# A graph kernel's step in another order, its score row spread through DRAM, its 512-column products halved

## The reference, cut to what matters

```python
def L0(X, A, Wv, bv, aw, ab, Wk, bk):        # K = 3
    Xw = X @ Wv + bv
    sj, si = Xw @ aw[:d, 0], Xw @ aw[d:, 0]
    e = leaky_relu(sj[:, None, :] + si[:, :, None] + ab[0], 0.2)
    alpha = A * exp(e)
    T = alpha / (sum(alpha, -1, keepdims=True) + 1e-12)
    H, Xk = 0, X
    for k in range(3):
        H = H + Xk @ Wk[k] + bk[k]
        Xk = T @ Xk
    return relu(H)

def gcn(x, adj, W, b):
    return adj @ (x @ W) + b

h = relu(layernorm(x));  x = x + L0(h, adj, ...)
h = relu(layernorm(x))
x = x + gcn(relu(gcn(relu(gcn(h, adj, W1, b1)), adj, W2, b2)), adj, W3, b3)
```

## Time and profile before

| what | value |
|---|---|
| median of 3 runs | 836.76 us (836.75 to 837.14) |
| the profiled execution | 837.53 us |
| its span, first to last instruction | 835.4 us |
| TensorE busy | 818.7 us, 98%, 6219 matmuls |
| VectorE busy | 718.0 us, 86% |
| ScalarE busy | 684.0 us, 82% |
| GpSimd busy | 506.8 us, 61% |
| mean granted TensorE clock | 0.997 of full |

### The profile page before, as it was taken

One profiled execution on the slowest core, in us unless ns is written; L12 is line 12 of the kernel. 1 busy time (PEld: TensorE's weight loads), 2 busy tenths in 40 slices (PEclk: granted clock), 3 DMA queues, 4 the chain that ended last, 5 costly groups with the idle time before them and its releaser, 6 DMA issues.

```text
span 835.4 us, 20996 instructions
## 1 busy us (share of the span) xinstructions
PE 818.7 (98%) x6219; PEld 772.0 (92%) x6219; DVE 718.0 (86%) x2001; ACT 684.0 (82%) x1673; POOL 506.8 (61%) x591
## 2 busy tenths in 40 slices
PE   7899999999999999999999999999999999999996
PEld 6799999999999999999999999999999999999995
DVE  6989889888889889889889889889888889889882
ACT  4788888888888888888888888888888888888774
POOL 3475665665665665665665665665665665665553
PEclk9999999999999999999999999999999999999999
DMA  7144334334344334334334334334334344344101
GB/s 195 43 99 107 86 95 103 91 94 104 88 95 102 92 93 103 92 93 110 84 93 108 87 93 106 87 94 106 88 94 105 85 97 109 83 95 102 46 27 38
DMA packets 245064, 77.54 MB, mean 93 GB/s; under 512 B 202324, under 2 KB 237016, under 8 KB 244952
## 3 DMA queue, kind: packets, MB, share of 16 engines
q1 hardware_dynamic: 243864, 75.16, 37.5%
q10 hardware_dynamic: 1088, 1.05, 0.4%
HBM read 43.39 MB, written 32.77 MB: 91 GB/s over the span
## 4 chain that ended last, share of the span: by engine, by line
PE 95%; ACT 1%; DVE 1%; DMA 1%; issue 1%; POOL 1%; ACTq 0%; DVEq 0%; POOLq 0%
PE bank L984 44%; PE bank_p L984 37%; PE bank_turned L984 7%; PE bank_T L984 5%; PE bank_T L1003 2%; DMA w_raw<-in_L_gnn_Wk 1%; POOL w_p_lo L422 0%; ACT y_full L614 0%; ACT h L490 0%; POOL y__lo L392 0%; PE bank_p L1160 0%; ACT y__hi L614 0%; DVE stats L693 0%; DVE alpha L766 0%; ACT y_hi L569 0%
## 5 line engine op out<-in xcount | busy, mean ns | idle before, releaser
L392 POOL TENSOR_TENSOR y__lo<-y_full,y__hi 128x256 fp32r<-128x256 f32 x256 | 183.6, 737 | 131.4 <-ACT y_full L614 131.4
L383 POOL TENSOR_TENSOR rstd<-veps,minus_half 128x2 f32<-128x2 f32 x128 | 111.6, 872 | 184.9 <-DVE veps L710 184.9
L984 PE MATMUL bank_p<-w_p_hi,h0T_hi 128*128 128x258 f32 (+1 forms) x512 | 176.3, 361 | 0.2 <-DVE y_full L795 0.2
L984 PE MATMUL bank_p<-w_p_lo,h0T_hi 128*128 128x258 f32 (+1 forms) x512 | 165.7, 339 | 0.0
L984 PE MATMUL bank_p<-w_p_hi,h0T_lo 128*128 128x258 f32 (+1 forms) x512 | 142.5, 340 | 0.0
L984 PE MATMUL bank<-w_gcn_hi,y__hi 128*128 128x256 f32 x512 | 130.2, 290 | 2.1 <-ACT y__hi L614 1.3
L984 PE MATMUL bank<-w_gcn_lo,y__hi 128*128 128x256 f32 x512 | 123.7, 278 | 0.0
L614 ACT ACTIVATE y__hi<-bank,bias_col 128x256 fp32r<-128x256 f32 x256 | 119.9, 468 | 3.6 <-PE bank L984 3.5
L614 ACT ACTIVATE y_full<-bank,bias_col 128x256 f32<-128x256 f32 x256 | 120.6, 471 | 0.0
L984 PEld LDWEIGHTS bank_p<-w_p_hi,h0T_hi 128*128 128x128 f32 x512 | 97.1, 190 | 6.5 <-issue 0.4
L984 PEld LDWEIGHTS bank_p<-w_p_lo,h0T_hi 128*128 128x128 f32 x512 | 97.6, 191 | 6.0
(11 more groups left out here) (100 smaller groups left out, 2285.4 us busy)
## 6 DMA issues: line engine op xcount, KB each, us to landing
x_in<-in_x SPq DMA_DIRECT2D x64, 256.0 KB, 3.0
x_new<-x_out SPq DMA_DIRECT2D x64, 256.0 KB, 2.2
h_rows<-h SPq DMA_DIRECT2D x61, 256.0 KB, 2.0
h_blocks<-h_rows SPq DMA_DIRECT2D x244, 64.0 KB, 2.6
adj_blocks<-in_adj SPq DMA_DIRECT2D x256, 32.0 KB, 2.0
w_raw<-in_L_gnn_Wk ACTq DMA_DIRECT2D x3, 256.0 KB, 6.9
w_raw<-in_L_gnn_W SPq DMA_DIRECT2D x3, 256.0 KB, 3.5
wv_raw<-in_L_gnn_Wv ACTq DMA_DIRECT2D x1, 256.0 KB, 3.8
```

The source lines that it names most:

```text
L383: pool.tensor_tensor(rstd[n][k % 2][:], veps[n][k % 2][:], minus_half[:], ALU.pow)\
L392: pool.tensor_tensor(y[n][1][:, c], y_full[n][:, c], plain(y[n][0][:, c]), ALU.subtract)\
L984: return pe.matmul(dst, stationary, moving, start=start, stop=stop, skip_group_check=True)
```

## The change

- The score row no longer goes through two transposes on TensorE but, from pair 3 on, through DRAM: SyncE writes one column of uv as 256 single numbers (`write_scores`) and reads them back broadcast to 128 partitions (`read_scores`); the logits read that tile in SBUF instead of bank_T.
- TensorE's order becomes p2 of a, ay of b, z1 of c, z3 of d, p01 graph 0 of a, s2 of c, p01 graph 1 of a, z2 of c, m of b, ap of a, s3 of c. z1 thus moves from the end of a round behind ay of the next. Rounds 0 to 2 keep the transposes; the filling in the last rounds is dropped.
- Each 512-column product of p01 is two of 256 with the same left operand.
- The lists of ScalarE, VectorE, GpSimd and SyncE are reordered to match. y1 is signalled graph by graph, and the high part of p2 waits graph by graph. ay runs its low part last and waits for y1_lo only there. s3, and the low parts of s2 and s3, wait chunk by chunk. GpSimd waits for y1_lo ahead of adjT_lo.

The diff, cut to its core:

```diff
+            def write_scores(i, k):
+                sp.wait_ge(uv_made, i + 1)
...
+                sp.dma_start(v_rows[k % 2].rearrange("g (n o) -> n g o", o=1), uv[k % 2][:, :, 1:2],
+                             allow_slow_non_contiguous=True).then_inc(v_out[k % 2], 16)
+            def read_scores(i, k):
+                sp.wait_ge(v_out[k % 2], scores_seen(i))
...
+                sp.dma_start(v_bc[k % 2][:], v_rows[k % 2].rearrange("(o g) n -> o g n", o=1)
+                             .to_broadcast([P, G, P])).then_inc(v_landed[k % 2], 16)
...
+                if spread is not None:
+                    write_scores(i, k)
+                    read_scores(i, k)
...
+                if b is not None:
+                    y1_high(b, kb)
+                if d is not None:
+                    s3_high(d)
                 if a is not None:
                     scores_copy(a, k)
                     p2_high(a, k)
+                if (n := next_norm(i)) is not None and after(i, 3):
+                    first_norm(n, n % ROUND)
+                if c is not None and i != 3:
+                    layer_result(0, c)
+                if (n := here(i, -1)) is not None and n > ON_TENSOR + 1:
+                    hT_high(n, n % ROUND)
+                if a is not None and a >= SPREAD_ON_TENSOR:
+                    logits(a, k)
+                    exponentials(a, k)
+                if c is not None:
+                    s2_copy(c)
+                if b is not None and after(i, 3):
+                    norm(b, kb)
                 if a is not None:
                     aT_high(a, k)
+                    if after(i, 2):
+                        p1_copy(a, k, 0)
                 if c is not None:
                     layer_result(1, c)
                 if a is not None:
                     p1_copy(a, k, 1)
...
+                if c is not None and after(i, 3):
+                    m_low(c)
+                if b is not None and after(b, 1):
+                    y1_low(b, kb)
+                if b is not None:
+                    p0_bias(b, kb)
+                if d is not None and after(d, 1):
+                    s3_low(d)
                 if b is not None:
                     h_sum(b, kb)
                     residual(b, kb)
                     x1_statistics(b, kb)
+                if nxt is not None and nxt > ON_TENSOR:
+                    turn_rows(nxt, kn)
...
-                        last = matmul(bank_p[:, g, :], h0T[k % 2][a][:, g, c, :], w_p01[b][:, c, :],
-                                      c == 0 and (a, b) == (HI, HI), c == C - 1 and a == LO)
+                        for n in range(2):
+                            cols = slice(n * D, (n + 1) * D)
+                            last = matmul(bank_p[:, g, cols], h0T[k % 2][a][:, g, c, :], w_p01[b][:, c, cols],
+                                          c == 0 and (a, b) == (HI, HI) and n == 0, c == C - 1 and a == LO)
...
+                if b is not None and after(i, 3):
+                    ay_product(b, kb)
+                if c is not None and after(i, 4) and not tail(i):
+                    z1_product(c)
+                if d is not None:
+                    z3_product(d, kd)
+                if a is not None and (first(i) or after(i, 3)):
+                    p01_product(a, k, 0)
+                if c is not None:
+                    s2_product(c)
                 if a is not None:
                     p01_product(a, k, 1, (0,))
                     p01_product(a, k, 1, (1,))
+                if c is not None:
+                    z2_product(c, kc)
+                if b is not None:
+                    m_product(b, kb)
+                if a is not None:
                     ap_product(a, k)
                 if c is not None:
                     s3_product(c)
```

More of the change, by code:

```diff
@@ L43 @@
 ON_TENSOR = 3
+SPREAD_ON_TENSOR = 3
 LN_EPS = 1e-5
@@ L209, in gnn_kernel @@
         spread_done = sem("spread_done")
+        v_out = [sem(f"v_out{k}") for k in range(2)]
+        v_landed = [sem(f"v_landed{k}") for k in range(2)]
         z_made = sem("z_made")
@@ L622, in one @@
                     p01_weights_high()
[L623 to L628, removed]
+                if b is not None:
+                    y1_high(b, kb)
+                if second(i):
+                    first_norm(2, 2)
+                if d is not None:
+                    s3_high(d)
                 if a is not None:
@@ L640, in one @@
                         hT_high(2, 2)
+                if first(i) or second(i):
                     p1_copy(a, k, 0)
+                if a is not None and a >= SPREAD_ON_TENSOR:
[3 more added lines that the diff above has]
+                    s2_copy(c)
+                if i == ON_TENSOR:
+                    hT_high(ON_TENSOR + 1, 0)
+                if b is not None and after(i, 3):
+                    norm(b, kb)
                 if i == 2:
                     adjT_high(0, 0)
-                if b is not None:
+                if b is not None and not after(i, 3):
                     norm(b, kb)
@@ L942, in one @@
                     attention(a, k)
+                if d is not None:
+                    finish(d, kd)
+                if a is not None and after(i, 2):
+                    p2_low(a, k)
                 if second(i):
                     hT_low(2, 2)
-                if nxt is not None and nxt >= ON_TENSOR:
+                if nxt == ON_TENSOR:
                     turn_rows(nxt, kn)
@@ L948, in one @@
                     aT_low(a, k)
-                if d is not None:
-                    finish(d, kd)
+                if (n := next_moments(i)) is not None:
+                    shift(0, n, n % ROUND)
                 if nxt is not None:
                     turn_adj(nxt, kn)
+                if second(i):
+                    m_low(b)
                 if a is not None:
@@ L1020, in h_low_ready, with times_weights @@
                     pe.wait_ge(hT_lo, i - ON_TENSOR + 1)
-            def times_weights(hT, rows, w, cols, dst, starts, passes=(False, True)):
-                steps = [(g, c, a, b) for low in passes for g in range(G) for c in range(C)
+            def times_weights(hT, rows, w, cols, dst, graphs, starts, passes=(False, True)):
+                steps = [(g, c, a, b) for low in passes for g in graphs for c in range(C)
                          for a, b in PARTS if (a == LO) == low]
@@ L1073, in ay_product @@
             def ay_product(i, k):
-                pe.wait_ge(y1_lo, i + 1)
-                pe.wait_ge(z_made, i + 1)
-                for g in range(G):
-                    for a, b in PARTS:
+                pe.wait_ge(y1_hi, i + 1)
+                pe.wait_ge(z_made, min(i + 1, SPREAD_ON_TENSOR))
+                if after(i, 1):
+                    pe.wait_ge(h_made, i)
+                for a, b in ((HI, HI), (LO, HI), (HI, LO)):
+                    if b == LO:
+                        pe.wait_ge(y1_lo, i + 1)
+                    for g in range(G):
                         last = matmul(ay_ps[:, g, :], aT[k % 2][a][:, g, :], y1[k % 2][b][:, g, :],
-                                      g == 0 and (a, b) == (HI, HI), a == LO)
+                                      g == 0 and (a, b) == (HI, HI), b == LO)
                 last.then_inc(ay_done, 1)
@@ L1115, in z1_product, with low_by_chunk @@
                 last.then_inc(z_done[0], 1)
+            def low_by_chunk(n, i, w, dst):
+                for c in range(C):
+                    pe.wait_ge(y_lo[n], C * i + c + 1)
+                    for g in range(G):
+                        last = matmul(dst[g], y[n][LO][:, c, g, :], w[HI][:, c, :], False, c == C - 1)
+                return last
             def s2_product(i):
```

210 lines of the change are left out of this document (112 added, 98 removed).

## The result

The changed kernel takes 1457.02 us (median of 4 runs, 1454.05 to 1461.24) against 836.91 (836.75 to 837.14): ratio 1.741, 95% interval 1.738 to 1.7445. The forecast was 819, range 812 to 838. The changed kernel is slower by 620 us, far outside the range, and far beyond the 885 given to the rival that named the cause.

What follows compares the result with a forecast made beforehand. TensorE was taken to bound the kernel, never waiting in a steady round. From the profiled 837.5 us, -19.5 for 61 shorter rounds and +1.0 for the ends gave 819.0 us, range 812 to 838.

Steps and rivals of the forecast that it cites:

- the rival that named the cause: The DRAM round trip of the score row becomes the new bound: slower, 885 us at 2.8 us a half; chance 0.16.
- What bounds the kernel now: Steady rounds: TensorE never waits, 12.53 us busy of 12.53; only its matmul sum or a new wait moves the time.
- The sum of the new round on TensorE: TensorE's matmul start distances per round: 12.21 us against 12.53, so -0.32, or -19.5 us in 61 rounds.
- The term for the halving: p0/p1 on TensorE: 24 products at z1's 0.1133 us, 2.72 against 2.80, -0.08 us a round.
- The price of the round trip: SyncE's write and read of the score row: 2.0 us each plus 0.1 hand-over, 4.1 us, covered up to about 4.6.
- the bound of 6.5: Upper bound given for the DRAM round trip of the score row; the lower was 4.0 us.
- rival A: Loop through the DRAM trip, 7.6 + D, sets the round: 849 us at D = 5.1, 885 at 5.7; chance 0.16.
- D: Time of the score row's round trip through DRAM, write, read and hand-over, ahead of the logits; forecast 4.1 us.
- Does the new order keep TensorE fed: Walk through the engines' queues: nothing stalls by the sum, but all covers are only 0.2 to 0.5 us thick.
- rival B: A 0.2 us cover (s3's low parts, z1's results, alpha) missed by 0.1 to 0.25 us each round: 825 to 834; chance 0.20.
- the lock with alpha: VectorE's alpha beside GpSimd's h0T_lo: 1.25 us instead of 0.69, ending about 8.4 instead of 8.2, before aT_hi's 8.8.
- Ends: First and last rounds: round 1 adds 0 (-1 to +1), the end +0.6 and +0.4; +1.0 us in all.

Runs made afterwards that it cites:

- order_shift: order_only with the second norm's shift moved right behind the statistics of x and the first norm's variance guard behind finish; 837.05 us, ratio 0.9992.
- split_only: The kernel before with only the 512-column products of p0/p1 halved to 256 columns; 837.9 us, ratio 1.001.
- order_shift_512: order_shift with the 512-column products left whole; 837.87 us, ratio 1.001.
- write_apart: The changed kernel with the 256 four-byte pieces written 512 bytes apart and the read taking a KB of bias bv; 870.51 us.
- read_apart: read_only with each partition reading its own KB of x instead of all 128 the same one; 872.24 us.
- read_only: The changed kernel with the score row written in rounds 3 and 4 alone, the read kept in each round; 877.5 us.
- after: The profile of the changed kernel itself, with nothing further altered; 1457.02 us, ratio 1.741 to the kernel before.
- filled: The changed kernel with 64 idle-filling transposes in TensorE's wait ahead of z2, from round 4 on; 1340.11 us.
- order_only: The changed kernel without the DRAM round trip: score transposes stay on TensorE behind z3, new order and halved products kept; 861.56 us, ratio 1.028.
- n_major: The changed kernel with the DRAM score row laid out node by node instead of graph by graph, same 256 four-byte pieces; 1335.09 us.

## Why the prediction was wrong, point by point

**What bounds the kernel now: right.** TensorE without idle; only a smaller sum or a new wait could move the time, and a new wait did.

**The sum of the new round on TensorE: right but for one term.** 12.21 was forecast without the transposes. With them, 0.23, it is 12.44, and order_shift measured 12.447. The term for the halving was too large: -0.08 was taken from z1's rows, 0.02 and 0.00 were measured. The Trainium skill's 262 for 518 cycles (TensorE: Matmul & The Clock Gate, Back-to-back issue gap), by the prediction's estimate +1.8 us, was nearer: split_only shows +1.1 with nothing within its interval, order_shift against order_shift_512 -0.8; the rows had said -4.9. The trace had a second sign: the first pair of a group costs 0.33 whatever its form, so part of the 12 products could not gain.

**The price of the round trip: the step that failed.** "I take 2.0 each" came from rows that were near in the wrong respect. The write of h is a write to DRAM, but in long rows; the bias columns are 4-byte pieces, but read from DRAM. Neither has 4-byte pieces *into* DRAM side by side, and that they lie side by side makes the price: write_apart writes the same pieces apart in 1.6 us (median), under the forecast's 2.0, where the changed kernel takes 7.9. So the bound of 6.5 was a bound on other transfers. The text said that no row showed a small write to DRAM and yet closed the range at 2.8 a half; a range that honoured it had to stay open above. The read was mis-sized too, at 2.0: it lands after 5.1 (median), of which 2.1 is the read, 1.0 that all read one KB, and 2.0 comes with the write ahead of it (read_apart, read_only, after). The Trainium skill's rule of read, modify and write below 512 bytes (DMA: Bandwidth & Descriptors, Specifications) had spoken for rival A; write_apart's pieces are as small, and its 1.6 us show nothing extra.

**Rival A: right mechanism, wrong size.** Its loop holds: 7.6 + D gives 20.5 where filled measured 20.7. With the changed kernel's mean D, 12.84, it gives 20.4, and the wait adds what no case had: TensorE's clock falls to 1.2 GHz for z2, m, ap and part of s3, 1.95 us a round by filled. 7.6 + 12.84 + 1.95 = 22.4 of a mean round of 22.63. Had the sum been made with the bound of 6.5, it would still have said 14.1 and about 935.

**Does the new order keep TensorE fed: wrong by 0.38 us a round, hidden behind the trip.** "All covers are 0.2 to 0.5 us thick" was the right worry, and rival B the right kind of loss. The text named the lock with alpha, and looked no further than that instruction. Measured: alpha beside h0T_lo costs the round nothing (order_shift), but a 0.17 us guard that nobody waits for is stretched to 1.09 us and stands ahead of the shift that m's chain needs. Had the trip been free, order_only says about 861 us, slower, not 825 to 834: 12.82 - 12.447 = 0.37 in 59 rounds is 22 us, and the ends add to it.

**"In its own rows SyncE's queue otherwise idle": true, and of no use.** The DMA engines were 2% busy during the write, and the wait was as long as it was.

**Ends: too small.** +1.0 was forecast; order_shift shows +2.6 in the first rounds and +3.5 behind the last uv. The first lies in round 3, where TensorE waits 0.94 us for hb and 0.86 for p_lo; for the second, the new place of ay and z1 behind p2 is the likely cause, which no run took apart. Net of the earlier first uv that is +3.9, most of the 4.9 that the order gains.

**What would show it.** Logits waiting for the DMA, TensorE waiting for s2: named for A, and found.

## What to carry to other kernels

Before you price a transfer by a row of the trace, compare direction, piece size and the distance of the pieces at the far side; if no row shares all three, its cost is open above, and the change is to be judged by how many us of cover stand in its loop. Small pieces written to DRAM were cheap here apart, or as one 16-byte row of each partition; but the whole trip still took 4.6 us with the first and 5.7 with the second (medians of D), and reading the score row back from pieces 512 bytes apart was not tried. When a list of steps is reordered, look for small two-port instructions of VectorE that now meet a long GpSimd product, and at what stands behind them in the queue, not at whether anyone waits for them.

## What the runs showed of the hardware beyond that

- 256 pieces of 4 bytes written to 1 KB of DRAM take 6.3 to 9.9 us to complete (medians 7.9 in after, 6.9 in n_major), 512 bytes apart 1.6 us (write_apart, median).
- A KB read by 128 partitions at once takes 3.1 us (read_only), 128 different KBs 2.1 (read_apart), the KB written just ahead of the read 5.1 (after) or 4.4 (n_major); the loads of adjacency go from 2.1 (read_apart) to 4.2 us (after).
- TensorE, idle for 8 us in each round, comes back at 1.2 GHz (granted clock 0.50): eight fp32 products in 1.87 us instead of 0.99 (z2, after against filled). 64 transposes for nothing in that wait keep 2.4 GHz, and save 117 us (1457 to 1340).
- A VectorE instruction of 0.17 us took 1.09 us behind a GpSimd product that had started 0.22 us before it.
